# A fused attention and mixture-of-experts block on one core: the second norm, the router and x2 move from the batch loop into the feed-forward's token tiles

## The reference

```python
h = concat(patches @ W.T + b, txt)
h = h + attention(layernorm(h))
h = h + ffn(layernorm(h))
# attention: 3 heads of 64, scores times a decay table, softmax, times v,
#   one group norm per batch and head (over all tokens of the batch), times Wo
# ffn: logits = x @ router_w.T (16 experts); softmax; the top 8, renormalised = comb
#   out = sum over experts e of comb[:, e] * (gelu(x @ w1_e) @ w2_e)
#   8 experts are 128 wide and 8 are 256 wide: 24 width tiles of 128
```

## Time and profile before

| | us |
|---|---|
| median of 3 runs | 898.36 (895.91 to 899.88) |
| the profiled execution, its own time | 898.34 |
| its span, first to last instruction | 896.5 |
| TensorE busy | 823.7 (92%) |
| VectorE busy | 578.1 (64%) |
| ScalarE busy | 498.9 (56%) |
| GpSimd busy | 88.7 (10%) |
| mean granted TensorE clock | 0.962 of full speed |

### The profile page before, as it was taken

The page is one execution under the profiler, slowest core; times in us unless marked ns, Lnnn a source line. Parts: engine busy times, 40 slices in busy tenths (PEclk is TensorE's granted clock), DMA queues, the critical chain, the costliest instruction groups (busy, mean ns, idle before and its releaser), DMA issues.

```text
span 896.5 us, 13902 instructions
## 1 busy us (share of the span) xinstructions
PE 823.7 (92%) x4360; PEld 671.8 (75%) x4360; DVE 578.1 (64%) x1586; ACT 498.9 (56%) x1151; POOL 88.7 (10%) x164
## 2 busy tenths in 40 slices
PE   5779999999999995675999999999999999999997
PEld 2758878797887874454777788888888888888885
DVE  6647788888888774682565555555556555555654
ACT  1457778887778884432454544445445454544543
POOL 3111031220203111160000000000000000000000
PEclk9779999999999997777999999999999999999999
DMA  8300010102101027534233343333334223332420
GB/s 237 117 18 19 1 57 21 55 20 75 48 28 55 20 75 276 185 106 148 58 90 82 84 106 72 100 88 78 94 71 116 72 78 94 83 105 72 102 86 18
DMA packets 50277, 74.20 MB, mean 83 GB/s; under 512 B 4178, under 2 KB 40498, under 8 KB 50098
## 3 DMA queue, kind: packets, MB, share of 16 engines
q1 hardware_dynamic: 50226, 73.57, 29.3%
HBM read 58.77 MB, written 14.79 MB: 82 GB/s over the span
## 4 chain that ended last, share of the span: by engine, by line
PE 62%; issue 19%; POOL 5%; DVE 4%; ACT 3%; POOLq 3%; DMA 2%; DVEq 0%; ACTq 0%; SPq 0%
PE ps L1116 58%; PE ps L1254 2%; ACT xn L514 2%; POOL w_lo L444 2%; DMA x_all<-x_dram 2%; DVE act_lo L832 1%; POOLq L421 1%; PE ps L1154 1%; POOL w_lo L491 1%; POOLq L454 1%; DMA gate<-comb_dram 1%; DVE act L1068 1%; ACT pt L501 1%; ACT act L724 1%; DVE h L1090 0%
## 5 line engine op out<-in xcount | busy, mean ns | idle before, releaser
L1068 DVE TENSOR_TENSOR act<-act,gate 128x480 f32<-128x480 f32 (+1 forms) x216 | 146.3, 678 | 218.3 <-ACT act L724 207.9
L724 ACT ACTIVATE act<-ps 128x480 f32<-128x480 f32 (+1 forms) x216 | 124.7, 578 | 261.8 <-PE ps L1116 259.8
L1116 PE MATMUL ps<-x_all,w_hi 128*128 128x480 f32 (+1 forms) x648 | 217.3, 390 | 0.6 <-SPq L253 0.6
L1116 PE MATMUL ps<-x_all,w_lo 128*128 128x480 f32 (+1 forms) x432 | 168.3, 390 | 0.0
L832 DVE TENSOR_TENSOR act_lo<-act,act_hi 128x480 fp32r<-128x480 f32 (+1 forms) x216 | 145.2, 672 | 0.1
L1116 PEld LDWEIGHTS ps<-x_all,w_hi 128*128 128x128 f32 x648 | 123.7, 191 | 23.2 <-SPq L253 1.3
L501 ACT ACTIVATE act_hi<-act 128x480 fp32r<-128x480 f32 (+1 forms) x216 | 130.3, 603 | 9.7 <-DVE act L1068 9.7
L1116 PE MATMUL ps<-act_hi,w_hi 128*128 128x480 f32 (+1 forms) x216 | 86.4, 400 | 17.5 <-DVE act_lo L832 16.1
L1116 PEld LDWEIGHTS ps<-x_all,w_lo 128*128 128x128 f32 x432 | 82.7, 191 | 14.3
L1116 PE MATMUL ps<-pt,v 68*128 68x512 f32 (+5 forms) x288 | 84.8, 445 | 0.0
L1116 PE MATMUL ps<-act_lo,w_hi 128*128 128x480 f32 (+1 forms) x216 | 83.6, 387 | 0.0
(11 more groups left out here) (189 smaller groups left out, 1287.3 us busy)
## 6 DMA issues: line engine op xcount, KB each, us to landing
gate<-comb_dram SPq DMA_DIRECT2D x112, 240.0 KB, 3.4
gate<-comb_dram SPq DMA_DIRECT2D x32, 256.0 KB, 3.4
x_dram<-x SPq DMA_DIRECT2D x7, 822.0 KB, 4.0
x_all<-x_dram SPq DMA_DIRECT2D x7, 720.0 KB, 4.6
w_raw<-w SPq DMA_DIRECT2D x8, 384.0 KB, 3.5
h_dram<-h SPq DMA_DIRECT2D x8, 384.0 KB
h<-h_dram SPq DMA_DIRECT2D x7, 360.0 KB, 4.8
out<-h SPq DMA_DIRECT2D x7, 360.0 KB, 3.4
```

Of the source, the lines that this page charges most:

```text
L724: a.activation(act[j % 3][:, 0:n], ps[:, j % 4, 0:n], ACT.Gelu_apprx_tanh).then_inc(gelu_done, 1)
L1068: dve.tensor_tensor(act[j % 3][:, 0:n], act[j % 3][:, 0:n], gate[e % 4][:, 0:n], ALU.mult).then_inc(gated, 1)
L1116: return pe.matmul(dst, w, x, start=start, stop=stop)
```

## The change

The router's part leaves the batch loop. It is made per token tile: for tile 0 in `body(7)`, for tile t+1 beside the steps of tile t, in a fixed place of each engine's order (below). h comes back from DRAM for it (three `res` buffers, also used for the final sum), x2 of a tile stays in SBUF (two buffers) and is no longer stored to DRAM, and comb is still stored and read back as gates. The logits take x2 as the weights (12 matmuls with 32 columns a tile), so that they come out with tokens on partitions and `logits_transpose` and `logits_copy` are gone; a sum of two parts is added in `router_shift`.

`drain` and the barrier are gone: TensorE goes from `body(7)` to `up(0)`, `up(1)` and `project(6)`, and head 2, group norm and `project` of batch 7 run beside the steps of tile 0. GpSimd splits all of w2, in eight parts of three width tiles, with the group norm's coefficients between parts 3 and 4. Its first part waits for batch 7's last exponentials.

Phase B has two `up` banks in tile 0, three later (bank 3 is the router's). From step 24 on TensorE's order is `up(j+3)`, `down(j)` and ScalarE's is `gelu(j+2)`, `act_round(j)`; in tile 0 it is `up(j+2)`, `down(j)` and `gelu(j+1)`, `act_round(j)`. VectorE's order stays.

TensorE's places beside tile t (after `down` of step k): `out_transpose(t-1)` k=1; `x2_transpose(t+1)` k=5 and 7; `logits` k=9; `comb_transpose` k=13. In tile 0 (before `down`): the rest of batch 7's attention at k=0, 1, 2, 4 and 8, then tile 1's router at k=11, 13, 15 and 17 (ScalarE's exponential at k=16, VectorE's `router_choose` at k=16).

The diff, cut to its core:

```diff
@@ banks and the order of the up projection @@
-W2_PART = NW // 4
+W2_PART = 3
+def down_banks(t):
+    return 4 if t % 2 else 6
+def up_bank(j):
+    return j % 2 if j < NW else j % 3
@@ SyncE @@
-            def body(b, tail, router, more):
+            def body(b, tail, later, more):
+                if not more:
+                    sp.wait_ge(h_stored, 32 * (B - 3))
+                    for t in range(3):
+                        load_res(t)
...
-                if router:
-                    store_x2(b - 2, x2)
-                    store_ct(b - 2)
+                if later:
                     store_h(b - 2)
...
+            def load_w2(p):
+                if p >= 2:
+                    sp.wait_ge(w2_split, p - 1)
+                sp.dma_start(w2_raw[p % 2], w2[:, p * W2_PART:(p + 1) * W2_PART, :]).then_inc(ld_w2[p % 2], 16)
...
+            store_ct(0)
+            sp.wait_ge(ct_stored, 16)
+            gates(0, 0, 4)
+            load_w2(2)
+            load_w2(3)
+            store_h(LB - 1)
+            gates(0, 4, 5)
+            load_w2(4)
+            gates(0, 5, 6)
+            load_w2(5)
+            gates(0, 6, 7)
+            load_w2(6)
+            gates(0, 7, 8)
+            load_w2(7)
+            gates(0, 8, 12)
+            store_h(LB)
+            gates(0, 12, 15)
+            store_ct(1)
+            gates(0, 15, 16)
@@ GpSimd, behind the batch loop @@
-            gn_coefficients(B - 1)
-            second_norm(B - 2)
...
+            for p in range(4):
+                split_w2(p)
+            gn_coefficients(LB)
+            for p in range(4, W2_PARTS):
+                split_w2(p)
+            for t in range(1, NTT):
+                second_norm(t)
@@ ScalarE, tiles 1 to 8, after act_round of step k @@
+                if k == 0:
+                    acc_copy(t - 1)
...
+                if k == 3:
+                    second_norm(t + 1, (0, 1))
+                elif k == 4:
+                    second_norm(t + 1, (2, 3))
+                elif k == 6:
+                    x2_round(t + 1, 0)
+                elif k == 8:
+                    x2_round(t + 1, 1)
+                elif k == 11:
+                    logits_exp(t + 1)
+                elif k == 14:
+                    comb_copy(t + 1)
@@ ScalarE, tile 0, after act_round of step k @@
+                if k == 0:
+                    pt_copy(LB, 2, (0, 1))
+                elif k == 1:
+                    pt_copy(LB, 2, (2, 3))
+                elif k == 3:
+                    o_copy(LB, 1, 2)
+                elif k == 6:
+                    y_round(LB, 0)
+                    y_whole(LB, 0)
...
@@ VectorE, tiles 1 to 8, after act_rest of step k @@
+                if k == 1:
+                    second_norm(t + 1)
+                elif k == 6:
+                    x2_rest(t + 1, 0)
+                elif k == 8:
+                    x2_rest(t + 1, 1)
+                elif k == 10:
+                    router_shift(t + 1)
+                elif k == 12:
+                    router_choose(t + 1)
@@ VectorE, tile 0 @@
+                if k == 1:
+                    second_norm(1)
+                elif k == 3:
+                    gn_partial(LB)
+                elif k == 5:
+                    gn_variance(LB, 4)
+                elif k == 7:
+                    y_rest(LB)
+                elif k == 9:
+                    add_attention(LB, (4, 5, 2))
...
@@ TensorE @@
+            def logits(t, bank=U_BANK):
...
+                for g in range(SEG):
+                    c = slice(g * r, (g + 1) * r)
+                    x = [x2[t % 2][:, i, c] for i in range(3)]
+                    near, rest = [rw[:, i, :, :].rearrange("p i e -> p (i e)") for i in range(2)]
+                    last = series(ps[:r, bank, 2 * E * g:2 * E * (g + 1)], [(x[0], near), (x[1], near), (x[2], rest)])
...
-            drain(B - 1, B - 2)
-            end_of_phase_a(pe)
...
-            for j in range(NTT * NW):
-                if j + 2 < NTT * NW:
-                    up(j + 2)
-                down(j)
...
+            up(0)
+            up(1)
+            project(LB - 1, (4, 5, 3))
+            for j in range(STEPS):
+                if j < NW - 2:
+                    up(j + 2)
+                elif j == NW - 2:
+                    up(j + 2)
+                    up(j + 3)
+                elif j + 3 < STEPS:
+                    up(j + 3)
+                if j < NW:
+                    beside_first(j)
+                down(j)
+                if j >= NW:
+                    beside(*divmod(j, NW))
```

More of the change, by code:

```diff
@@ L173, in early_fusion @@
[L173 to L191, removed]
+        w_raw = sb("w_raw", [P, 2, W2_PART * 256])
@@ new lines, in early_fusion @@
+        decay, xn, xa_hi, xa_lo, xb, q01_hi, q01_lo, k01_hi, k01_lo, q2, k2_hi, k2_lo, sc0, sc1, pr1 = both[0]
+        w2_hi, w2_lo, w2_r, *others = both[1]
+        sc = [sc0, sc1]
+        act_hi, act_lo, act = others[0:3], others[3:6], others[6:8]
+        act.append(sb("act2", [P, TW]))
+        v = sb("v", [P, NT, 3 * P])
+        pt = sb("pt", [P, 4, 512])
+        x2_0 = sb("x2_0", [P, 3, TW], F32R)
+        (pr0,), (x2_1,) = overlay([("pr0", [P, PW], F32)], [("x2_1", [P, 3, TW], F32R)])
@@ L243, in iterations @@
         def iterations(eng, body):
-            body(0, tail=False, router=False, more=True)
-            body(1, tail=True, router=False, more=True)
+            body(0, tail=False, later=False, more=True)
+            body(1, tail=True, later=False, more=True)
             with eng.Fori(2, B - 1) as b:
[L248 to L254, removed]
+                body(b, tail=True, later=True, more=True)
+            body(B - 1, tail=True, later=True, more=False)
+        LB = B - 1
+        STEPS = NTT * NW
         def tokens(ap, b, I):
@@ L637, in body @@
                     pt_copy(t, 2)
-                if router:
-                    norm_apply(u, rstdb, nmrb, ln2_rstd, xn2, ln2_normed)
+                if not more:
+                    second_norm(0)
                 exps(b, 0, (0,))
@@ L737, in acc_copy @@
                     a.wait_ge(outt_done, t)
-                copy(out_a[:, 0:n], ps[:, 4 + 2 * (t % 2), 0:n]).then_inc(acc_a_copied, 1)
-            gelu(0)
-            gelu(1)
-            round_w2(0, W2_HEAD)
-            act_round(0)
-            act_round(1)
-            round_w2(W2_HEAD, W2_PART)
-            gelu(2)
-            for j in range(2, NTT * NW):
-                if j + 1 < NTT * NW:
-                    gelu(j + 1)
+                else:
+                    a.wait_ge(y_lo, nth(LB, 2, 2))
@@ L1004, in body @@
                 normalise(b, 0)
-                if router:
-                    x2_rest(u, 1, x2)
+                if not more:
+                    x2_rest(0, 0, 6)
+                    x2_rest(0, 1, 7)
                 if tail:
@@ L1011, in body @@
                     gn_variance(t)
-                if router:
-                    router_shift(u)
-                    router_choose(u)
+                if not more:
+                    router_shift(0, 2)
+                    router_choose(0)
                 apply_decay(b, 2)
@@ L1329, in comb_transpose, with x2_transpose @@
[L1329 to L1333 removed]
+            def x2_transpose(t, c, bank=U_BANK):
+                r = width(t) // SEG
+                if c == 0:
+                    pe.wait_ge(xn2_ready, t + 1)
+                    apart(pe, "pe")
+                    if t >= 2:
+                        pe.wait_ge(ct_copied, t)
+                    elif t == 1:
+                        pe.wait_ge(o_copied, nth(LB, 2, 2))
+                elif t:
+                    pe.wait_ge(x2_lo, nth(t, 2, 1))
+                for g in range(SEG):
+                    last = pe.transpose(ps[:, bank, g * r:(g + 1) * r], xn2[:r, g, c * P:(c + 1) * P], ident[:r, :r])
+                last.then_inc(x2t_done, 1)
@@ L1334, in comb_transpose, with body @@
+            def comb_transpose(t, bank=U_BANK):
+                r = width(t) // SEG
+                pe.wait_ge(comb_ready, t + 1)
+                for g in range(SEG):
+                    last = pe.transpose(ps[0:E, bank, g * r:(g + 1) * r], comb[:r, g, :], ident[:r, :r])
                 last.then_inc(ct_done, 1)
-            def body(b, tail, router, more):
-                t, u = b - 1, b - 2
-                qk(b, tail, router)
+            def body(b, tail, later, more):
+                t = b - 1
+                qk(b, tail, later)
@@ L1341, in body @@
                     probs_transpose(t, 2, (0, 1))
-                scores(b, 0, tail, router)
+                scores(b, 0, tail, more)
                 if tail:
```

747 lines of the change are left out of this document (357 added, 390 removed).

## The result

| | before | after |
|---|---|---|
| median, in runs on one chip | 898.45 (895.91 to 899.88) | 882.97 (882.00 to 883.26) |
| ratio, 95% interval | | 0.983 (0.981 to 0.985) |
| the profiled execution | 898.34 | 882.96 |
| its span | 896.5 | 881.2 |

A forecast was written before the change was run, and what follows sets the result against it. TensorE was taken to bound the kernel, alone setting phase B's tiles. Batch loop -14.8, boundary -30.1 and tiles +39.2 summed to -5.7 us against 898.34: 892.6, say 892.5, range 876 to 909.

The forecast's parts named there:

- the loop's period: Batch loop without the router: a body takes 36.3 us instead of 39.2, 2.9 less in each of five periods.
- the hole at `down(6)`: Tile 0: TensorE waits 9.7 us because expert 7's gate queues behind `load_w2(6)`, which waits for the fifth split.
- two waits a tile: Tiles 1 to 7: `down(12)` waits 1.65 us for ScalarE's table loads, `down(13)` 1.0 for `router_choose`.
- the rivals: Swallowed waits (chance 0.21), doubled table-switch cost (0.06), clock falling in every tile (0.05), batch loop staying as long (0.08).
- The first rival: Waits beside the tiles are swallowed by `gelu` running ahead: 874 us at full price, 883 at half; chance 0.21.
- term 3: Tiles 1 to 7 get longer by 5.6 us each, 2.9 of TensorE work plus waits: +39.2 us.
- The room: Idle time in a tile's step that covers added work: ScalarE 1.13 us, VectorE 0.97, and 0.15 before `down`.
- term 2: Boundary from the end of `attend(7,1)` to tile 1's first `down`: 125.7 us shrinks to 94.1 plus 1.5, -30.1.
- the first hole: TensorE idle 3 to 4 us before tile 0's `down(0)`; 1.5 us put down for half clock, between 0 and 5.
- Small waits: Minor TensorE waits in tile 0, from `gn_partial` and tile 1's router: 2 us.
- the 67.4: TensorE's work from `down(0)` to tile 1's first `down`, in us: `down`, `up`, `attend`, `project`, transposes and tile 1's router.
- Term 1: Batch loop: bodies 2 to 6 lose 2.9 us each and `body(7)` 0.3, -14.8 us in all.

The follow-up runs named there:

- all three waits away: Changed kernel with six w2 parts split before batch 7's coefficients, the exponential made from Tanh, and `router_choose` halved over two steps: 859.98 us, ratio 0.957.
- the second set: The changed kernel run once more without any edit, to see what differs from run to run: 883.72 us, ratio 0.982 to the kernel before.
- split order: Changed kernel with six instead of four of the eight w2 parts split ahead of batch 7's group norm coefficients: 873.02 us, ratio 0.971.
- no exponential: Changed kernel with a copy in place of the router's exponential for tiles 1 to 8, so ScalarE keeps its tables: 871.58 us, ratio 0.969.
- `router_choose` in two: Changed kernel with `router_choose` of tiles 2 to 8 cut in two on VectorE, at steps 12 and 13: 875.99 us, ratio 0.975.
- the loop experiment: Changed kernel with `x_transpose`'s ten transposes made four times over in the hardware loop's bodies, 30 more TensorE instructions a period: 897.27 us, ratio 0.998.

## Why the prediction was off by a factor

The sign, the mechanisms and the places were right: the loop's period, the hole at `down(6)` with its releaser and its half clock, two waits a tile, 18 table loads for 16 or 17 (one at the start, nine for gelu, eight for the exponential). None of the rivals happened; that the half price of the first one, 883, is the time measured is coincidence, as its waits stayed. What failed is the size: a sum of +39.2, -30.1 and -14.8, whose 5.7 is less than the 9.6 by which its terms were off together. Three of the four errors had one sign. The step that failed in both traces of the changed kernel by the most is term 3: a lead that was priced at nothing, and two waits that were put too long.

- **Term 3, tiles 1 to 7: +34.5 for +39.2, the step that failed.** TensorE's own 2.9 a tile was right. A tile without a wait takes 56.29 with the lead (all three waits away), so some 56.6 without it, 2.9 over 53.7; 24 instructions at 0.102 are 2.4 of that. The waits were 1.46 and 0.79 to 1.06, 2.3 together, where I had 1.65 and 1.0. The room that I took off each was a little too small. And the lead of one step, which I named only as a reason for a rival, I priced at nothing; it gave 0.35 a tile, through steps, not through the two waits. 0.3 and 0.35 over seven tiles are 4.6 of the 4.7.
- **Tile 8: -1.4 for 0.** I counted 25 `up` behind `down(0)`, the one of the lead among them, in term 2, and didn't take it off tile 8, which has 237 matmuls for 242. That is 1.1; a book-keeping slip.
- **Term 2, the boundary: 90.6 for 94.1 + 1.5.** In the second set's trace it takes 92.0, so 3.6 of the 5.0 hold in both. Until `down(0)` 11.2 for 12. The hole 8.49 for 9.7: from `gvar` on, coefficients 1.7 (1.9 put down), the split 2.6 (2.9), two issues 0.8 (0.9), the gate 3.1 until `weigh` starts (4.0), `weigh` and the rest 2.3 (1.7), less the 2.1 that TensorE still had (1.7). Small waits 1.0 for 2 (two of 0.76 and 0.24). The clock fell behind this hole for 10 us, 6 of them with TensorE at work, so 3, as taken. Behind the first hole it didn't fall in this trace (1.5 put down), but did in the second set's, from 329.5 to 336.3. What is left, 0.5, is in the 67.4 of TensorE's work, where I had multiplied wrongly: 245 matmuls at 0.234 are 57.3, and not 57.8.
- **Term 1, the loop: -13.3 for -14.8.** The bodies gave 3.2 each, not 2.9, since 30 instructions cost 0.104 and not 0.1: -15.9. Body 7 took 0.1 more instead of 0.3 less, by a clock fall of its own (309.3 to 312.8): it takes 38.0 here, and 37.1 in the three traces without that fall (split order, no exponential, `router_choose` in two), 0.8 less than before. The rest, +2.4, is the clock in this one execution: two bodies 2.8 longer, with half clock at 121.6 to 128.4 and 268.4 to 275.2, against a `body(0)` that is 4.6 shorter and a first transpose 1.2 later. I had no term for that, in either direction. The scalar and vector work that leaves is misread in the prediction as some 6 us each: by the two windows it is 4.7 and 8.9 with `project`'s, by the loop experiment 4.2 and 7.1; it enters no term.
- **The rule of the Trainium skill** (ScalarE: Activation LUTs, What ACT_TABLE_LOAD costs), 1380 ns of drain beside each load, would by my estimate have given 22 us more. This case's trace doesn't agree: the rows show 0.02 or less ahead of and behind a load in the middle of a full queue, and so it is at all 17 loads behind the start. In the experiment without the exponential two loads are worth 1.8 a tile; with that drain they would be worth 2.8 more. Going by the row was right here.
- **The first rival,** that the lead swallows the waits, expected a gain from the lead, and there is one, but not in the waits: with or without the lead they are the same within 0.1. What was said against it in the prediction shows in the trace: act has three buffers, and the second gelu behind the loads stands for 0.79 until `act_lo`, the last reader of its buffer:

```profile
620.55 0.57 ACT L710 ACTIVATE act<-ps 128x480 f32<-128x480 f32 x1 [0.79 <-DVE act_lo L869]
```

## What to carry to other kernels

When a forecast is the small difference of large terms, each term's own error is what the forecast is made of: carry it on to the sum, and count every instruction that moves past the border of a stretch on both sides. A queue written out by hand that holds a load behind a split and a gate behind the load ties three engines together; moving two splits ahead of an unrelated wait took 6.7 us off TensorE's waits. Before a second transcendental function goes into the middle of a loop, look whether it can be made from one that the loaded tables already have.

## What was not expected of the hardware

- On ScalarE, Tanh between two gelus took no table load: 2 loads in the whole kernel for 18, and 0.25 us for 120x64 elements, as Exp's 0.26.
- A transpose of 120 or 128 columns costs TensorE 0.102 to 0.104 put into a full stream, though each one's record shows 0.27, and it made no difference whether 24 stand together in a tile or 30 in a body.
- The granted clock falls by chance in the batch loop too, where TensorE waits for no more than 1.8 us a body. The traces of one kernel, the changed one, show `body(0)` at 34.5 and at 39.9, and bodies 2 and 6 at 38.8 and at 36.0. The two go together: the trace with the order of before (the lead taken away) again has 34.5 with bodies 2 and 6 at 38.8, its falls within 0.2 us of the same places, and the traces with `body(0)` at 37.2 or more have no fall in these two bodies (one has it in body 5). What decides between the two no run here shows. A body moves by 2.8 to 5.5 us with it, and with few runs a median may move too: a difference under 3 us is better read from starts in the traces.
